# A scan with a feed-forward block behind it: matmuls dealt singly, a shorter start, and GpSimd in the preparation

## The chip, the cores and the metric

One NeuronCore of a Trainium2 chip. The metric is the device time of one execution in microseconds (us), the median over the runs shown.

## The reference

The input x has 16 sequences of 128 steps and 256 features. It drives a recurrence whose state q, p starts at cond. Each of the 128 steps is a Runge-Kutta step of fourth order, so each asks four times, one after the other, for the derivative:

```
def _derivative(q, p, drive, coupling, bias):
    i_couple = jnp.tanh(q) @ coupling.T
    dq = q - q ** 3 / 3.0 - p + drive + i_couple + bias
    dp = EPSILON * (q + ALPHA - BETA * p)
...
logits = x @ W_router.T                       # x is here the trace of q, 2048 tokens of 256
sh = _silu_and_mul(x @ Ws_gate_up, I_SH) @ Ws_down
gu = jnp.einsum('th,ehi->eti', x, We_gate_up)
h = _silu_and_mul(gu, I_MOE)
eo = jnp.einsum('eti,eih->eth', h, We_down)   # 8 experts, the two best weighted by softmax
```

The clipped q after every step is the token that goes through the feed-forward network (FFN): a shared part of 704 hidden columns and eight experts of 176. All are computed and weighted, and the sum is added to x.

## The kernel before

**Scan.** The 512 evaluations are called stages. 32 stages (8 steps) are a block; there are 16 blocks of 128 tokens. n counts stages over all blocks, st within one. In stage n TensorE (PE) runs `couple`: three small matmuls with a scaled identity add the three bf16 parts of x (line 554), eight multiply the high half of the coupling matrix and its rest by `th_hi` (565), and four use `th_lo` (571). ScalarE (ACT) makes `th_hi` and the float32 tanh (439, 440) from the new q; VectorE (DVE) subtracts them to `th_lo` (820), forms the cubic terms and `force`, and at line 848 adds PE's sum into the next q. That is a closed loop through the engines, 512 times.

**FFN.** The FFN of block f runs behind the scan of blocks f+1 and f+2. Tables name the stage at which each engine issues each piece. There are 17 tiles of 128 hidden columns. `UP_AT` gives two stages per tile: 6 matmuls for gate and 6 for up (629). ACT applies silu (`SILU_AT`, 480), DVE multiplies (`HIDE_AT`, 895), GpSimd (POOL) weights by the router's factor (`WEIGH_AT`, 963), PE multiplies with `w_down` (`DOWN_AT`, 646, two float32 matmuls per tile, four records in the trace). On PE this work stands between line 571 of one stage and line 554 of the next. A unit below is the time of one float16 matmul with 128 columns.

**Fillers.** `WARM` puts up to 6 matmuls whose result is not used (558) into a stage of the steady blocks that has fewer than 11 units. They stand between the x parts and the high half. In block 0, stages 16 to 18 have 8 fillers each (664), behind their coupling.

**Start.** SyncE (SP) issues all loads; DVE waits for `cf` and the identity, takes the largest coupling entry (690), PE turns it to one row (507), DVE reduces (692), PE widens it (511), five small DVE operations make a power of two `scale` and its inverse, two larger ones (713, 714) make the two float16 halves `c16`, and ACT and DVE prepare x of block 0 (394, 730, 734).

**Preparation of w_up.** During blocks 0 and 1 w_up is split into two float16 halves. `HI_AT` (ACT, line 417) makes the high half of a tile. The low half is either formed by DVE (`LO_AT`, 772) in rows of 128 columns (four rows a tile), or by PE and ACT: two matmuls per row give the rest in PSUM (`REST_AT`, 539 and 540) and ACT rounds it (`ROUND_AT`, 422). DVE does 9 tiles and PE with ACT 8.

**End.** After the last stage the FFN of block 15, and what is left of block 14, run in the same order without the scan between them. Then two additions and a store end the kernel.

Of the kernel before, what the change touches and what calls it, by code (L numbers as in the profile page):

```python
# [23 lines left out]
U32 = mybir.dt.uint32  # L24
ALU = mybir.AluOpType
# [47 lines left out]
def err(z):  # L73
# [13 lines left out]
UP_AT = [(2, 2), (3, 3), (4, 4), (6, 6), (8, 8), (9, 10), (11, 11), (12, 12), (13, 13), (15, 15), (16, 16), (17, 18),  # L87
         (20, 20), (22, 22), (23, 24), (26, 26), (27, 28)]
SILU_AT = [u[1] + 1 for u in UP_AT]
# [4 lines left out]
WEIGH_AT = [17, 18, 19, 21, 22, 23, 25, 26, 27, 29, 30, 31, 32, 37, 38, 39, 42]  # L94
# [3 lines left out]
assert len(UP_AT) == len(HIDE_AT) == len(DOWN_AT) == len(WEIGH_AT) == TILES and len(SPREAD_AT) == GROUPS  # L98
assert all(h > s for h, s in zip(HIDE_AT, SILU_AT))
assert all(w > max(s, c) and d > w for w, s, c, d in zip(WEIGH_AT, HIDE_AT, COPY_AT, DOWN_AT))  # L100
assert DOWN_AT[-1] < FINISH_AT[0] and FINISH_AT[-1] <= STAGES + DOWN_AT[0]


def units(st):

    halves = sum(u.count(st) for u in UP_AT)
    downs = DOWN_AT.count(st) + DOWN_AT.count(st + STAGES) + (st == 0)
    return 6 * halves + 8 * downs + 4 * SPREAD_AT.count(st)


WARM = [min(6, max(0, 11 - units(st))) for st in range(STAGES)]
# [5 lines left out]
HI_AT = {17: (0, 0, 4), 18: (1, 0, 4), 19: (2, 0, 4), 20: (3, 0, 4), 21: (4, 0, 4), 24: (5, 0, 4), 25: (6, 0, 4),  # L117
         28: (7, 0, 4), 29: (8, 0, 4), 30: (9, 0, 4), 33: (10, 0, 2), 37: (10, 2, 4), 38: (11, 0, 4), 41: (12, 0, 2),
         42: (13, 0, 4), 45: (12, 2, 4), 49: (14, 0, 2), 50: (14, 2, 4), 52: (15, 0, 4), 53: (16, 0, 4)}
REST_AT = {19: ((1, 0), (1, 1)), 20: ((1, 2), (1, 3)), 21: ((2, 0), (2, 1)), 22: ((2, 2), (2, 3)),  # L120
# [3 lines left out]
ROUND_AT = {22: 1, 23: 2, 26: 3, 27: 5, 31: 7, 34: 9, 40: 10, 47: 11}  # L124
REST_TILES = list(ROUND_AT.values())
LO_AT = {18: ((0, 0, 1),), 19: ((0, 1, 2),), 20: ((0, 2, 3),), 21: ((0, 3, 4),),
# [18 lines left out]
LO_DONE = {tile: so_far(LO_AT, n, i) for n, parts in sorted(LO_AT.items()) for i, (tile, _, _) in enumerate(parts)}
assert sorted([*LO_DONE, *REST_TILES]) == list(range(TILES))
assert sum(len(x) for x in REST_AT.values()) == ROWS * len(REST_TILES)
W_STEPS = 7
HALF = STEPS // 2
X_FIRST = [14, 15]  # L150
X_AT = [1, 3]
SPLIT_FIRST = [2, 5]
SPLIT_NEXT = [17, 19, 20]
SPLIT_AT = [20, 24, 28]
# [5 lines left out]
def program(nc, x, cond, coupling, bias, w_up, w_down, w_route, identity, spread, iota, e_base, out):  # L160
    ctx = ExitStack()
    with ctx:
# [33 lines left out]
        w_sum = sb("w_sum", [P, W_PARTS])  # L196
        most1 = sb("most1", [1, 2])
# [8 lines left out]
        p_first = sb("p_first", [P, KC, B])  # L206
# [46 lines left out]
        in_cf = sem("in_cf")  # L253
        in_core = sem("in_core")
        in_const = sem("in_const")
        in_x = sem("in_x")
# [4 lines left out]
        setup_a = sem("setup_a")  # L261
        zeroed = sem("zeroed")
        x_biased = sem("x_biased")
        x_split = sem("x_split")
# [8 lines left out]
        w_rounded = sem("w_rounded")  # L273

# [30 lines left out]
        SETUP_V = 12  # L305
# [23 lines left out]
        def _(sync):  # L329
            sync.dma_start(cf[:], coupling).then_inc(in_cf, 16)  # L330
            sync.dma_start(ident[:], identity).then_inc(in_cf, 16)
            sync.dma_start(bias_s[:], bias).then_inc(in_core, 16)
            sync.dma_start(xs[:, 0:STEPS], x[:, 0:STEPS]).then_inc(in_x, 16)
            sync.dma_start(q_raw[:], cond).then_inc(in_core, 16)
            sync.dma_start(q_trace[:, :, STEPS - 1, :], cond).then_inc(in_core, 16)
            sync.dma_start(p_first[:], cond).then_inc(in_core, 16)
            for i in range(ROWS):
                sync.dma_start(wf[:, i // 2, i % 2], w_up[:, i // 2, i % 2]).then_inc(in_w[i], 16)
            sync.dma_start(xs[:, STEPS:T], x[:, STEPS:T]).then_inc(in_x, 16)
# [684 lines left out]
```

## Time and profile before

| | |
|---|---|
| median of 3 runs | 655.67 us (655.66, 655.67 and 658.51) |
| the profiled execution, its own time | 658.68 us |
| its span, first to last instruction | 656.9 us |
| busy: PE, DVE, ACT, POOL | 97%, 93%, 56%, 30% of the span |
| mean granted TensorE clock | 0.992 |

Device time and span of the profiled execution differ by 1.8 us, which lie around the span. Busy time of PE counts overlapped matmuls whole, so 97% does not mean that PE could do no more: what a stage waits for is to be read from the order of starts.

### The profile page before, as it was taken

The numbers are of one execution on the slowest core, as the hardware profiler recorded it, in microseconds if no ns is written. First come the engines' busy times: TensorE is split into PE (matmuls) and PEld (weight loads), VectorE is DVE, ScalarE is ACT, GpSimd is POOL, SyncE is SP. The second block draws the span as 40 slices with busy tenths as digits, with TensorE's granted clock in tenths as the row PEclk, the third lists the DMA queues.
The fourth block names the chain that finished last, engine by engine and source line by source line (L and its number), as shares of the span: only waits on it lengthen the run. The fifth ranks groups of instructions, "written<-read, shape, count | busy, mean of one in ns | idle before, by whom it ended". The sixth has DMA issues, their size and how long they took to land.

```text
span 656.9 us, 33948 instructions
## 1 busy us (share of the span) xinstructions
PE 637.9 (97%) x12839; PEld 610.6 (93%) x12839; DVE 614.0 (93%) x4540; ACT 365.4 (56%) x1880; POOL 194.0 (30%) x436
## 2 busy tenths in 40 slices
PE   3899999999999999999999999999999999999998
PEld 2689899999999999999999999999999999999997
DVE  6998999999999999999999999999999999999951
ACT  4776655555555555556555555555556555554643
POOL 0002133242323334232333423233342323323244
PEclk9997999999999999999999999999999999999999
DMA  7800000000000000000000000000000000000000
GB/s 297 279 2 2 4 2 4 11 3 11 4 11 3 3 12 2 12 2 12 3 4 10 4 12 3 11 4 2 12 4 11 3 12 2 4 12 3 11 3 17
DMA packets 9059, 13.65 MB, mean 21 GB/s; under 512 B 1568, under 2 KB 8032, under 8 KB 8256
## 3 DMA queue, kind: packets, MB, share of 16 engines
q1 hardware_dynamic: 8896, 11.50, 5.2%
q8 instruction: 100, 1.64, 1.0%
q14 instruction: 63, 0.52, 0.3%
HBM read 9.40 MB, written 2.10 MB: 17 GB/s over the span
## 4 chain that ended last, share of the span: by engine, by line
PE 90%; DVE 8%; DMA 0%; issue 0%; ACT 0%; POOL 0%; DVEq 0%; SPq 0%
PE up_ps L629 28%; PE down_ps L646 21%; PE coup_ps L565 15%; PE coup_ps L571 13%; PE coup_ps L554 5%; PE coup_ps L558 3%; PE route_ps L603 2%; DVE q L848 1%; PE route_ps L584 1%; DVE w L772 1%; DVE force L831 1%; DVE th_lo L820 1%; DVE square_ps L817 1%; DVE square_ps L813 1%; DVE p_sum L784 1%; DVE y L784 0%
## 5 line engine op out<-in xcount | busy, mean ns | idle before, releaser
L629 PE MATMUL up_ps<-q_hi,w 128*128 128x128 f16 x2176 | 236.4, 219 | 0.2 <-POOL q_lo L926 0.2
L963 POOL TENSOR_TENSOR hidden<-hidden,comb_s 128x128 f32<-128x128 f32 x272 | 123.3, 456 | 297.7 <-ACT th_hi L439 290.2
L439 ACT ACTIVATE th_hi<-q 128x32 f16<-128x32 f32 x384 | 88.1, 229 | 213.6 <-DVE q L848 211.9
L629 PE MATMUL up_ps<-q_lo,w 128*128 128x128 f16 x1088 | 199.7, 220 | 0.0
L565 PE MATMUL coup_ps<-th_hi,c 128*128 128x16 f16 x4096 | 180.7, 171 | 0.2
L646 PE MATMUL down_ps<-hidden,wd 128*128 128x128 f32 x1088 | 180.8, 290 | 0.0
L629 PEld LDWEIGHTS up_ps<-q_hi,w 128*128 128x128 f16 x2176 | 176.2, 98 | 0.7 <-POOL q_lo L926 0.4
L565 PEld LDWEIGHTS coup_ps<-th_hi,c 128*128 128x128 f16 x4096 | 138.8, 96 | 4.6
L646 PEld LDWEIGHTS down_ps<-hidden,wd 128*128 128x128 f32 x1088 | 141.9, 191 | 0.0
L571 PE MATMUL coup_ps<-th_lo,c 128*128 128x16 f16 x2048 | 131.4, 173 | 0.4 <-DVE th_lo L820 0.3
L480 ACT ACTIVATE act_s<-up_ps,unscale 128x128 f32<-128x128 f32 x272 | 98.9, 364 | 13.8 <-PE up_ps L629 10.1
L629 PEld LDWEIGHTS up_ps<-q_lo,w 128*128 128x128 f16 x1088 | 105.9, 97 | 0.1
L554 PE MATMUL coup_ps<-xb,ident_u 128*128 128x32 bf16 x512 | 92.9, 181 | 10.1 <-DVE q L848 4.4
L571 PEld LDWEIGHTS coup_ps<-th_lo,c 128*128 128x128 f16 x2048 | 85.7, 97 | 16.2 <-DVE th_lo L820 0.7
L848 DVE SCALAR_TENSOR_TENSOR q<-coup_ps,c_un,force 128x32 f32<-128x32 f32 x384 | 96.3, 251 | 4.6 <-PE coup_ps L571 2.5
L820 DVE TENSOR_TENSOR th_lo<-th_ps,th_hi 128x32 f16<-128x32 f32 x512 | 97.8, 191 | 1.0 <-ACT th_ps L440 1.0
L554 PE MATMUL coup_ps<-x_rest,ident_u 128*128 128x32 bf16 x512 | 90.9, 178 | 0.0
L554 PE MATMUL coup_ps<-x_low,ident_u 128*128 128x32 bf16 x512 | 90.6, 177 | 0.0
L895 DVE TENSOR_TENSOR hidden<-act_s,up_ps 128x128 f32<-128x128 f32 x272 | 76.3, 281 | 13.2 <-ACT act_s L480 13.2
L813 DVE SCALAR_TENSOR_TENSOR square_ps<-q 128x32 f32<-128x32 f32 x384 | 76.6, 199 | 0.0
L817 DVE SCALAR_TENSOR_TENSOR square_ps<-square_ps,q 128x32 f32<-128x32 f32 x384 | 76.5, 199 | 0.0
L784 DVE SCALAR_TENSOR_TENSOR p_sum<-q,p_sum 128x32 f32<-128x32 f32 x384 | 71.0, 185 | 0.0
(107 smaller groups left out, 1098.8 us busy)
## 6 DMA issues: line engine op xcount, KB each, us to landing
wf<-in_w_up SPq DMA_DIRECT2D x4, 1056.0 KB, 8.3
wd<-in_w_down SPq DMA_DIRECT2D x1, 2048.0 KB, 21.0
out<-out_s SPq DMA_DIRECT2D x16, 128.0 KB, 2.2
xs<-in_x SPq DMA_DIRECT2D x1, 1920.0 KB, 17.3
sel<-in_spread SPq DMA_DIRECT2D x1, 408.0 KB, 17.1
cf<-in_coupling SPq DMA_DIRECT2D x1, 256.0 KB, 2.6
xs<-in_x SPq DMA_DIRECT2D x1, 128.0 KB, 2.4
ident<-in_identity SPq DMA_DIRECT2D x1, 64.0 KB, 2.5
```

Source lines behind the costliest of these rows:

```text
L439: nc.scalar.activation(th_hi[:], q[:], ACT.Tanh).then_inc(hi_ready, 1)
L480: nc.scalar.activation(act_s[:, j % 4, :], up_ps[(f * TILES + j) % UPS][:, 0:TOK], ACT.Silu, scale=unscale[:, 1:2]).then_inc(silu_ready, 1)
L554: nc.tensor.matmul(coup_ps[:, 0:CB], ident_u[:], piece, start=x == 0, stop=False, skip_group_check=True)
L565: nc.tensor.matmul(coup_ps[:, m * B:(m + 1) * B], c16[:, part, k, m * P:(m + 1) * P], th_hi[:, k, :], start=False, stop=False, skip_group_ ...
L571: last = nc.tensor.matmul(coup_ps[:, m * B:(m + 1) * B], c16[:, 0, k, m * P:(m + 1) * P], th_lo[:, k, :], start=False, stop=True, skip_gro ...
L629: last = nc.tensor.matmul(up_ps[(f * TILES + j) % UPS][:, h * TOK:(h + 1) * TOK], w16[:, part, k, h, j * P:(j + 1) * P], q[:, k, :], start ...
L646: last = nc.tensor.matmul(down_ps[:, m * TOK:(m + 1) * TOK], wd[:, j, m * P:(m + 1) * P], hidden[:, j, :], start=j == m == 0, stop=j == TI ...
L813: nc.vector.scalar_tensor_tensor(square, q, THIRD[k], q, ALU.mult, ALU.mult).then_inc(squared, 1)
L817: nc.vector.scalar_tensor_tensor(cubic, square, LINEAR[k], q, ALU.subtract, ALU.mult).then_inc(cubed, 1)
L820: nc.vector.tensor_tensor(th_lo[:], th, th_hi[:], ALU.subtract).then_inc(lo_ready, 1)
L848: nc.vector.scalar_tensor_tensor(q_raw[:] if k == 3 else q_in[k + 1][:], coup_ps[:, 0:CB].rearrange("p (m b) -> p m b", m=KC), c_un[:, (0, ...
L963: nc.gpsimd.tensor_tensor(hidden[:, j, :], hidden[:, j, :], comb_s[:, j, :], ALU.mult).then_inc(weighed, 1)
```

## The change

It has these parts.

1. `UP_AT` goes; `UPS_IN` says how many of the 204 up matmuls each stage issues, so a tile may begin or end within a stage. `DOWN_AT` gets a stage for each of the two down matmuls of a tile. Hide, spread and weigh stages move by a few places.
2. The fillers of the steady blocks and those of line 664 go. New ones stand at line 558 in stages 17 to 34 only: 10 minus 5 for each rest row of the stage before (and minus 8 for the router's stage), which is 10 at n = 17, 18, 21 and 22, 2 at n = 33, and none else.
3. The start: no turn and widen; one matmul of a matrix of ones with the row maxima gives a bound on them all. Three small operations for `scale` and its inverse. ACT loads cond and bias through its own queue, makes one half of the first `c16` part and the scaled identity; stage 0's tanh comes first. cond is loaded once instead of three times, and the identity is not waited for by the first reduction.
4. POOL splits x of blocks 0 and 1 into its three parts and adds the bias for blocks 1 and 2 (stages 1 to 13), which ACT and DVE did.
5. Low half of w_up: of 68 rows 36 come from PE and ACT (9 tiles), 23 from DVE, and 9 from POOL, which first makes the scaled row (`POOL_SCALE_AT`) and then subtracts (`POOL_LO_AT`). The rest rows of PE also use the bank `route_ps`.

```diff
-UP_AT = [(2, 2), (3, 3), (4, 4), (6, 6), (8, 8), (9, 10), (11, 11), (12, 12), (13, 13), (15, 15), (16, 16), (17, 18),
-         (20, 20), (22, 22), (23, 24), (26, 26), (27, 28)]
-HIDE_AT = [4, 7, 8, 10, 11, 12, 13, 14, 15, 18, 19, 21, 22, 25, 26, 29, 30]
+UPS_IN = [0, 0, 12, 8, 4, 8, 8, 8, 8, 8, 8, 8, 8, 10, 0, 11, 12, 8, 3, 8, 4, 8, 8, 8, 4, 8, 8, 8, 8, 0, 0, 0]
+HIDE_AT = [4, 7, 8, 10, 11, 12, 14, 15, 18, 19, 21, 22, 25, 26, 27, 29, 30]
-SPREAD_AT = [14, 17, 21, 25, 30]
+SPREAD_AT = [14, 17, 20, 24, 29]
-DOWN_AT = [18, 19, 21, 23, 24, 25, 27, 28, 29, 30, 31, 33, 37, 39, 41, 42, 46]
+DOWN_AT = [(18, 18), (19, 20), (21, 22), (23, 24), (25, 26), (27, 28), (29, 29), (30, 30), (31, 31), (31, 33),
+           (33, 35), (36, 36), (37, 38), (39, 40), (41, 42), (43, 44), (46, 46)]
...
-WARM = [min(6, max(0, 11 - units(st))) for st in range(STAGES)]
+WARM_FROM, WARM_TO = 17, STAGES + 3
+WARM = [max(0, 10 - 5 * len(REST_AT.get(n, ())) - 8 * (n == STAGES)) for n in range(WARM_TO)]
...
+REST_AT = {18: ((14, 0), (14, 1)), 19: ((14, 2), (14, 3)), 22: ((1, 0), (1, 1)), 23: ((1, 2), (1, 3)),
...
+           33: ((7, 0), (7, 1)), 35: ((7, 2),), 36: ((7, 3),), 38: ((10, 0),), 39: ((10, 1),), 40: ((10, 2),),
+           41: ((10, 3),), 42: ((13, 0),), 43: ((13, 1),), 44: ((13, 2),), 46: ((13, 3),)}
...
-         43: ((12, 0, 1),), 44: ((12, 1, 2),), 45: ((13, 0, 1),), 46: ((12, 2, 3),), 47: ((12, 3, 4),),
-         48: ((13, 1, 3),), 49: ((13, 3, 4),), 50: ((14, 0, 1),), 51: ((14, 1, 2),), 53: ((14, 2, 4), (15, 0, 1)),
-         54: ((15, 1, 2), (16, 0, 2)), 55: ((15, 2, 4), (16, 2, 4))}
+LO_AT = {17: (5, 0), 18: (5, 2), 19: (5, 3), 20: (8, 1), 21: (8, 2), 22: (8, 3), 23: (2, 1), 24: (2, 2), 25: (2, 3),
+         26: (0, 1), 27: (0, 2), 28: (0, 3), 29: (12, 0), 30: (12, 2), 31: (12, 3), 32: (11, 0), 41: (11, 2),
+         45: (11, 3), 48: (15, 0), 49: (15, 3), 52: (16, 1), 55: (16, 2), 56: (16, 3)}
+POOL_SCALE_AT = {17: (5, 1), 19: (8, 0), 22: (2, 0), 25: (0, 0), 27: (12, 1), 30: (11, 1), 37: (15, 2), 39: (15, 1),
+                 45: (16, 0)}
+POOL_LO_AT = {18: (5, 1), 21: (8, 0), 23: (2, 0), 26: (0, 0), 29: (12, 1), 31: (11, 1), 38: (15, 2), 42: (15, 1),
+              46: (16, 0)}
...
+X_AHEAD = {1: (0, 2), 2: (0, 3), 3: (1, "m0"), 5: (1, "m1"), 6: (1, 0), 7: (1, 1), 9: (1, 2), 10: (1, 3),
+           11: (2, "m0"), 13: (2, "m1")}
...
+            act.dma_start(q_raw[:], cond).then_inc(in_core, 16)
+            act.dma_start(bias_s[:], bias).then_inc(in_core, 16)
...
+                    act.wait_ge(setup_v, 4)
+                    nc.scalar.mul(c16[:, 0, 1], cf[:, 1], scale[:, 0:1]).then_inc(c_cast, 1)
+                    act.wait_ge(in_ident, 16)
+                    nc.scalar.mul(ident_u[:], ident[:], scale[:, 0:1]).then_inc(unit_cast, 1)
...
-            pe.wait_ge(in_cf, 2 * 16)
             pe.wait_ge(setup_v, 1)
-            turn(0).then_inc(setup_t, 1)
-            pe.wait_ge(setup_v, 2)
-            widen(0).then_inc(setup_t, 1)
+            nc.tensor.matmul(route_ps[:, 0:1], ones[:], most[:, 0:1], start=True, stop=True).then_inc(setup_t, 1)
...
-                if n > STAGES:
-                    for _ in range(WARM[st - 1]):
+                if WARM_FROM <= n < WARM_TO:
+                    for _ in range(WARM[n - 1]):
...
+                for i in range(UP_FROM[st], UP_FROM[st] + UPS_IN[st]) if st < STAGES else ():
+                    j, h, k, product = i // UP_MMS, i // (3 * KC) % 2, i // 3 % KC, i % 3
...
-                    if b == 0 and STAGES // 2 <= st < min(REST_AT):
-
-                        for _ in range(8):
-                            nc.tensor.matmul(up_ps[0][:, 0:P], c16[:, 0, 0, 0:P], c16[:, 0, 0, 0:P], start=True,
-                                             stop=True)
...
+            step(nc.vector.tensor_scalar(c16[:, 0, 0], cf[:, 0], scale[:, 0:1], None, ALU.mult))
+            step(rest_of_c(0))
+            dve.wait_ge(c_cast, 1)
+            step(rest_of_c(1))
...
+            split_x(0, 0)
+            split_x(0, 1)
+            pool.wait_ge(setup_v, 5)
...
+                    nc.gpsimd.tensor_scalar(w_scaled_row[:, 0:w.shape[-1]], w, scale[:, 1:2], None, ALU.mult
+                                            ).then_inc(w_pooled, 1)
...
+                    nc.gpsimd.tensor_tensor(w_lo, w_scaled_row[:, 0:w_lo.shape[-1]], w_hi, ALU.subtract
+                                            ).then_inc(w_pooled, 1)
...
+                    if n in X_AHEAD or n in POOL_SCALE_AT or n in POOL_LO_AT:
+
+                        pool.wait_ge(hi_ready, n + 1)
+                        prepare(n)
```

## Rows read from the trace of the kernel before

**Rows 1.** The page: the chain of work that ended last, by engine.

```profile
PE 90%; DVE 8%; DMA 0%; issue 0%; ACT 0%; POOL 0%; DVEq 0%; SPq 0%
```

**Rows 2.** The timeline (start us, duration us, engine, line, operation), two steady stages.

```profile
331.26 0.25 DVE L848 SCALAR_TENSOR_TENSOR q<-coup_ps,c_un,force 128x32 f32<-128x32 f32 x1
...
332.14 0.26 PE L571 MATMUL coup_ps<-th_lo,c 128*128 128x16 f16 x4
...
332.44 0.25 DVE L848 SCALAR_TENSOR_TENSOR q_raw<-coup_ps,c_un,force 128x32 f32<-128x32 f32 x1
...
333.65 0.25 DVE L848 SCALAR_TENSOR_TENSOR q<-coup_ps,c_un,force 128x32 f32<-128x32 f32 x1
```

**Rows 3.** The chain in order of time: twelve up matmuls, twice.

```profile
54.38 1.29 PE up_ps L629 x12
...
87.17 0.69 PE up_ps L629 x12
```

**Rows 4.** The timeline of PE alone: a stage with six ups and one tile of down.

```profile
335.76 0.25 PE L571 MATMUL coup_ps<-th_lo,c 128*128 128x16 f16 x4
...
336.20 0.66 PE L646 MATMUL down_ps<-hidden,wd 128*128 128x128 f32 x4
336.70 0.18 PE L554 MATMUL coup_ps<-xb,ident_u 128*128 128x32 bf16 x1
...
336.97 0.24 PE L571 MATMUL coup_ps<-th_lo,c 128*128 128x16 f16 x4
```

**Rows 5.** The timeline of DVE: q of stages 0, 30, 36, 63 and 511.

```profile
10.67 0.25 DVE L848 SCALAR_TENSOR_TENSOR q<-coup_ps,c_un,force 128x32 f32<-128x32 f32 x1
...
47.54 0.24 DVE L848 SCALAR_TENSOR_TENSOR q<-coup_ps,c_un,force 128x32 f32<-128x32 f32 x1
...
57.77 0.25 DVE L848 SCALAR_TENSOR_TENSOR q<-coup_ps,c_un,force 128x32 f32<-128x32 f32 x1 [0.41 <-PE coup_ps L571]
...
93.17 0.25 DVE L848 SCALAR_TENSOR_TENSOR q_raw<-coup_ps,c_un,force 128x32 f32<-128x32 f32 x1
...
628.81 0.25 DVE L848 SCALAR_TENSOR_TENSOR q_raw<-coup_ps,c_un,force 128x32 f32<-128x32 f32 x1
```

**Rows 6.** Windows of 1 us: start:end, length, busy of the engines, PEclk, DMA.

```profile
47.00:48.00 1.00, 1.00 (x17) 0.94 (x15) 1.00 (x9) 0.74 (x3) 0.00 (x0) 0.81 0.00 0
57.00:58.00 1.00, 1.00 (x25) 1.00 (x23) 0.59 (x6) 0.37 (x1) 0.30 (x1) 0.57 0.00 0
```

**Rows 7.** The timeline of the start.

```profile
3.67 0.69 DVE L690 TENSOR_REDUCE most<-cf 128x1 f32<-128x512 f32 x1 [1.93 <-DMA ident<-in_identity]
...
5.20 0.28 DVE L692 TENSOR_REDUCE most<-route_ps 1x1 f32<-1x128 f32 x1 [0.84 <-PE route_ps L507]
...
6.22 0.16 DVE L698 COPY most<-route_ps 128x1 f32<-128x1 f32 x1 [0.74 <-PE route_ps L511]
...
6.83 0.69 ACT L394 ACTIVATE xb<-xs,bias_c 128x128 f32<-128x128 f32 x2
...
7.16 0.49 DVE L713 TENSOR_SCALAR c<-cf,scale 128x512 f16<-128x512 f32 x1
...
7.68 0.75 DVE L714 SCALAR_TENSOR_TENSOR c<-cf,scale,c 128x512 f16<-128x512 f32 x1
```

**Rows 8.** The timeline of PE: fillers of stage 16 and what follows.

```profile
29.79 1.01 PE L664 MATMUL up_ps<-c 128*128 128x128 f16 x8
30.60 0.23 PE L554 MATMUL coup_ps<-xb,ident_u 128*128 128x32 bf16 x1
```

**Rows 9.** The timeline of PE: the last down matmuls.

```profile
649.98 3.79 PE L646 MATMUL down_ps<-hidden,wd 128*128 128x128 f32 x32
```

**Rows 10.** The timeline, then one line's instructions (min/median/max ns): POOL beside DVE.

```profile
82.63 0.46 POOL L963 TENSOR_TENSOR hidden<-hidden,comb_s 128x128 f32<-128x128 f32 x1 [1.22 <-ACT th_hi L439]
...
82.89 0.74 DVE L772 SCALAR_TENSOR_TENSOR w<-wf,scale,w 128x256 f16<-128x256 f32 x2
...
L772 DVE SCALAR_TENSOR_TENSOR w<-wf,scale,w x31: 343/345/479, 32.3 to 83.3; 128x128 f16<-128x128 f32 x28, 128x256 f16<-128x256 f32 x3
```

More of the change, by code:

```diff
@@ new lines, with in_order @@
+POOL_LO_AT = {18: (5, 1), 21: (8, 0), 23: (2, 0), 26: (0, 0), 29: (12, 1), 31: (11, 1), 38: (15, 2), 42: (15, 1),
+              46: (16, 0)}
+def in_order(table):
+    return [part for _, parts in sorted(table.items()) for part in parts]
+HI_ORDER = in_order(HI_AT)
+REST_ORDER = in_order(REST_AT)
+ROUND_ORDER = in_order(ROUND_AT)
+REST_TILES = list(REST_BANK)
+LO_ORDER = [part for _, part in sorted(LO_AT.items())]
+POOL_ORDER = [part for _, part in sorted(POOL_LO_AT.items())]
+assert POOL_ORDER == [part for _, part in sorted(POOL_SCALE_AT.items())]
@@ new lines, with rounds_done, parts_done, bank_rounds @@
+assert sorted(REST_ORDER + LO_ORDER + POOL_ORDER) == [(j, r) for j in range(TILES) for r in range(ROWS)]
+def hi_done(tile, row):
+    return max(i for i, (j, r0, r1) in enumerate(HI_ORDER) if j == tile and r0 <= row < r1) + 1
+def rounds_done(tile):
+    return max(i for i, part in enumerate(ROUND_ORDER) if part[0] == tile) + 1
+def parts_done(order, tile):
+    return max([i + 1 for i, part in enumerate(order) if part[0] == tile], default=0)
+def bank_rounds(bank):
+    return max(rounds_done(tile) for tile in REST_TILES if REST_BANK[tile] == bank)
@@ L545, in couple @@
                 if n == 0:
-                    pe.wait_ge(setup_v, 10)
+                    pe.wait_ge(setup_v, 3)
+                    pe.wait_ge(unit_cast, 1)
                 else:
@@ L561, in couple @@
                 pe.wait_ge(hi_ready, n + 1)
+                if n == 0:
+                    pe.wait_ge(setup_v, 6)
+                    pe.wait_ge(c_cast, 1)
                 for part in range(2):
+                    if n == 0 and part:
+                        pe.wait_ge(setup_v, 8)
                     for m in range(KC):
@@ L579, in ffn @@
                     pe.wait_ge(q_clipped, (f + 1) * STEPS)
-                    if not first_block:
+                    if first_block:
+                        pe.wait_ge(w_rounded, max(rounds_done(j) for j in REST_TILES
+                                                  if REST_BANK[j] == "route" and (j, 0) in REST_ORDER[:24]))
+                    else:
                         pe.wait_ge(comb_copied, f * TILES)
@@ L646, in ffn @@
+                for j in range(TILES):
+                    for m in range(KC):
+                        if DOWN_AT[j][m] == st:
+                            pe.wait_ge(weighed, f * TILES + j + 1)
+                            if j == m == 0:
+                                if first_block:
+                                    pe.wait_ge(w_rounded, bank_rounds("down"))
+                                else:
+                                    pe.wait_ge(out_ready, KC * f)
                             last = nc.tensor.matmul(down_ps[:, m * TOK:(m + 1) * TOK],
@@ L710, in _ @@
-            dve.wait_ge(setup_t, 2)
-            for x in range(5):
-                step(power(x, 0))
-            step(nc.vector.tensor_scalar(c16[:, 0], cf[:], scale[:, 0:1], None, ALU.mult))
-            step(nc.vector.scalar_tensor_tensor(c16[:, 1], cf[:], scale[:, 0:1], c16[:, 0], ALU.mult,
-                                                ALU.subtract))
-            step(nc.vector.tensor_scalar(ident_u[:], ident[:], scale[:, 0:1], None, ALU.mult))
-            for k in (0, 2, 3):
-                last = nc.vector.tensor_scalar(c_un[:, k:k + 1], unscale[:, 0:1], C[k], None, ALU.mult)
@@ L719, in _ @@
-            step(last)
-            dve.wait_ge(in_core, 4 * 16)
-            step(nc.vector.tensor_scalar(p_now[:], p_first[:], SHIFT, C[0] / Q_NEXT[0], ALU.subtract, ALU.mult))
-            assert done[0] == SETUP_V
+            dve.wait_ge(in_core, 2 * 16)
+            step(nc.vector.tensor_scalar(p_now[:], q_raw[:], SHIFT, C[0] / Q_NEXT[0], ALU.subtract, ALU.mult))
+            dve.wait_ge(tanh_ready, 1)
+            nc.vector.tensor_tensor(th_lo[:], th, th_hi[:], ALU.subtract).then_inc(lo_ready, 1)
@@ L768, in prepare @@
                                             ).then_inc(idents_ready, 1)
-                for j, r0, r1 in LO_AT.get(n, ()):
-                    dve.wait_ge(w_hi_ready, hi_done(j, r1 - 1))
-                    w, w_hi, w_lo = [x[:, r0:r1] for x in w_tile(j)]
+                if n in LO_AT:
+                    j, row = LO_AT[n]
+                    dve.wait_ge(w_hi_ready, hi_done(j, row))
+                    w, w_hi, w_lo = [x[:, row] for x in w_tile(j)]
                     nc.vector.scalar_tensor_tensor(w_lo, w, scale[:, 1:2], w_hi, ALU.mult, ALU.subtract
@@ L818, in scan_stage @@
                                                    ).then_inc(cubed, 1)
-                dve.wait_ge(tanh_ready, n + 1)
-                nc.vector.tensor_tensor(th_lo[:], th, th_hi[:], ALU.subtract).then_inc(lo_ready, 1)
-                if k == 0:
+                if n:
+                    dve.wait_ge(tanh_ready, n + 1)
+                    nc.vector.tensor_tensor(th_lo[:], th, th_hi[:], ALU.subtract).then_inc(lo_ready, 1)
+                if k == 0 and n:
                     dve.wait_ge(squared, n + 1)
```

311 lines of the change are left out of this document (178 added, 133 removed), and 11 rows, old and new, of tables (HI_AT, LO_AT, REST_AT).

## The prediction

> **What bounds the kernel now.** I read the page's chain first. It gives PE 90% [rows 1], which suggests that fewer or better packed matmuls pay everywhere. The timeline says otherwise. In a steady stage q starts at 331.26 and the next at 332.44, 1.18 us later; the one behind it, the first stage of a step, takes 1.21 [rows 2]. Within it PE's last four matmuls start at 332.14 and q 0.30 later. They had waited for th_lo, which comes through ACT and DVE from the q before. So the loop through three engines takes 1.18 whatever PE does in the gap, as long as PE is back in time. A step is 3 x 1.18 + 1.21 = 4.75 us, a block 38.0.
>
> How much PE may do in the gap: with six ups and one tile of down the period from line 571 to line 571 is 336.97 - 335.76 = 1.21, and there PE is the one that is late, by 0.03 [rows 4]. The down block took 0.50 of it (336.20 to 336.70). Twelve ups take 0.69, of which 0.02 is beyond twelve starts [rows 3], and leave the loop at 1.18: the stage from 331.26 to 332.44 comes behind twelve [rows 2]. So the limit lies near 0.80 us of work, 14 units, and the kernel is at it in a few stages per block.
>
> Then the times of q by stretch [rows 5]. Stage 0: 10.67. Stages 1 to 30: 36.87. Stages 31 to 36: 10.23. Stages 37 to 63: 35.40. The last 448 stages, 14 blocks: 535.64, or 38.26 a block. After the last q: 656.9 - 628.81 = 28.1. The windows of 1 us show why the third stretch is long: the granted clock falls at 47.6 to 0.50 (1.2 GHz) and is back at 57.9 [rows 6]; before it, PE had two stages with nothing but the coupling. Twelve ups cost 1.29 there instead of 0.69 [rows 3].
>
> **The change part by part.**
>
> *Start.* Now: largest entry at 3.67 for 0.69, first PE answer at 5.20 (0.84 after), second at 6.22, five small operations until 7.16 (0.19 each), 0.49 and 0.75 for the two halves [rows 7]. After: the reduction starts when cf is there; it was issued ahead of the identity, so I take 3.3 (bounds 2.9 and 3.67). It ends at 4.0, one PE answer at 4.85, two small operations, scale at 5.2, the third at 5.4. DVE casts half of c (0.26) and takes two halves of the rest (0.38 each): 6.45. PE's part and q follow 0.55 later: 7.0. Beside it: ACT has x with its bias 0.69 after its tanh, about 4.6; POOL's two splits, not seen before, I price at its 128x128 operation of 0.46 [rows 10]: 5.6; ACT casts and the scaled identity until 5.9. That cover is 0.4 to 0.8 us deep. Gain 10.67 - 7.0 = 3.7 (bounds 3.0 and 4.0; if POOL needed twice as long it would be 3.2). DVE's two x splits of stages 2 and 5 are gone too, 0.1.
>
> *Block 0 fillers.* Eight fillers cost 29.79 to 30.60, 0.81 at 1.2 GHz [rows 8], 0.10 each; at 2.4 GHz 0.057 [rows 3]. They used to stand behind the coupling, in the gap. The new ones stand between the x parts and the high half, that is on the loop. Ten cold ones end about 1.5 us after q where th_lo's matmuls used to start 0.88 after it [rows 2] and eight high-half matmuls (0.2) still have to come: +0.85 in stages 17 and 18 each, 1.7. The first rest rows at stage 18 are still partly cold: +0.4. At 21 and 22 the clock is up: ten take 0.57, +0.3 each, 0.6. Together 2.7. Today's block 0 has 36.87 against 35.6 for 30 undisturbed stages; some 0.6 of this are its 24 fillers. Net loss 2.1 (bounds 0.8, if the clock rises during stage 17, and 3.5, if it takes until 20).
>
> *The cold spell.* The new tables have rest rows or fillers in all but one stage from 17 to 33, so PE has no two empty stages; then come twelve ups. Stages 31 to 36 now cost 10.23; undisturbed 4 x 1.18 + 2 x 1.21 = 7.14. Gain 3.1, of which I leave 0.15 for ACT, which now rounds two halves at n = 33. So -2.95 against the profile (bounds 0 and 3.1).
>
> *Rest of block 1.* 35.40 for 27 stages against 32.0: 3.4 us are lost, because DVE's low rows (0.345 each [rows 10]) share stages with its hide operations and pile up at 53 to 55. After: eight DVE rows in block 1, none in a hide stage; single rest rows for PE beside 8 ups, 0.69/2 + 0.45 = 0.79, just at the limit; ACT at about 1.0 to 1.2 per stage. I leave 0.6 lost. Gain 2.75 (bounds 1.5 and 3.3). POOL's rows stand in stages where it had nothing.
>
> *Steady blocks.* The old fillers cost nothing: they stood in stages in which th_hi was not there yet. Their removal alone gives nothing. The even deal does: a stage now holds at most 12 ups or 8 ups and one down, 0.45 + 0.28 = 0.73 (half of 0.50, and 0.03 for changing over), under 0.80. 38.26 - 38.0 over 14 blocks is 3.3 us; I count five stages a block that are late by 0.03 as the one in rows 4, behind six ups and a tile of down, which is 2.1 of it, the rest are single late stages of another kind. Gain 2.2 (bounds 0.8 and 3.3). More is not to be had here, since the loop stays.
>
> *Tail.* No loop there; PE works without a gap until the last 32 records, which take 3.79 [rows 9], 0.114 each, 0.23 a down matmul. A block of 4 takes 0.50 [rows 4], so 0.05 is paid per change between ups and downs. After stage 511 block 14 has 15 down matmuls left instead of 12: +0.7. Single downs make 22 changes before the last up instead of 13: +0.4. Loss 1.1 (bounds 0.3 and 2.2).
>
> Sum: -3.7 - 0.1 + 2.1 - 2.95 - 2.75 - 2.2 + 1.1 = -8.5. Against the profiled execution: span 656.9 to 648.4, time 658.68 to 650.2.
>
> **The profile and the median.** The profiled execution is 3.0 us above the median, and one of the three runs (658.51) is at its height while two agree to 0.01. The only thing in the trace that costs 3 us at once is the cold spell, 3.1. I take it that the median run had none. Then the gain against the median lacks that term: 655.67 - (8.5 - 2.95) = 650.1. Both ways give the same time.
>
> **The rivals.** 0.5% of the time, about 3.3 us, is what a measurement can tell from no change.
>
> (a) The 3 us are the cost of being profiled, and the cold spell is in every run. Then 655.67 - 8.5 = 647.2. For it: profiled times stand above medians here. Against: 658.51 without a profile. Chance 0.13.
>
> (b) POOL and DVE get in each other's way. In 13 stages of blocks 0 and 1 both work on w_up; POOL starts when th_hi is ready and runs 0.46, DVE's low row starts 0.26 later [rows 10]; held up to POOL's end, q is 0.2 late in each: 2.6 us, 652.7. In the rows DVE's low rows started 0.26 into a POOL operation and took 0.74 for two; all 31 lie at 343 to 345 ns (479 for the double width), so nothing was held up. The Trainium skill, page "SBUF — State Buffer", section "Who interferes with whom", says that a DVE instruction with two SBUF inputs contends with a GpSimd instruction that reads SBUF, and that the loser waits for the whole instruction. By that rule the time would be this rival's; the trace does not agree. Chance 0.10.
>
> (c) The fillers come too late or too thin, and the clock stays at 1.2 GHz through block 0. Then ten stages with two rest rows each (0.69 warm, about 1.3 cold by the ratio of rows 3) cost 0.5 more each, and the first ups 3 more: 650.1 + 8 = 658, slower. Chance 0.05.
>
> (d) The clock falls in the steady blocks, where nothing fills a light stage any more. One fall costs 3.1. One is borne, two cancel the gain, from three on the kernel is slower; one per block would give 650 + 43 = 693. For it: stage 0 has only the router. Against: stages 29 to 1 hold about 12, 8, 12, 0 and 8 units beside the router where they now hold 8, 15, 8, 3 and 11, nearly as much, and it took two stages with the coupling alone to make it fall. Chance 0.07.
>
> **How the numbers follow.** The forecast, all terms as above, has 0.65; its own range, from the bounds of its terms taken one or two at a time, is 648 to 652.4, with 0.1 of it above 652.4. Faster by over 0.5% (under 652.4): 0.58 + 0.13 + 0.04 of (b) = 0.75. Slower by over 0.5% (over 658.9): most of (d) and half of (c), 0.09. Same: 0.16. The range that leaves no more than 2 in 10 out is 646.5 to 654.5: it takes in (a) and (b).
>
> **What would show it.** Start of q of stage 0 near 7.0. Stages 17 and 18 near 2.0 us, 21 and 22 near 1.5. PE clock 1.00 from stage 19 on, no fall near the turn of block 0. Stages 32 to 63 near 38.8 in all. Blocks 2 to 15 at 38.1. From the last q to the end 29.2. The sum is wrong if the steady blocks move by more than their 0.26, or if a 0.50 clock shows after stage 20.

## The result, and the profile after

The changed kernel takes 653.98 us, the median of 20 runs (650.95 to 661.84). The kernel before, run 20 times beside it, takes 658.5 (655.66 to 659.57). The ratio is 0.9937, 95% interval 0.9921 to 0.9952: faster by 0.6%. One run of the twenty, 661.84, counts as slow and is left out of the ratio. I had forecast 650.1, from 655.67 as the time before. The profiled execution took 656.32, with a span of 654.5; before it was 656.9. It lies 2.3 us above its own median.

The times of q in the changed kernel, stages 0, 30, 36, 63 and 511, from DVE's timeline, against [rows 5]:

```profile
7.36 0.25 DVE L907 SCALAR_TENSOR_TENSOR q<-coup_ps,c_un,force 128x32 f32<-128x32 f32 x1
...
50.96 0.24 DVE L907 SCALAR_TENSOR_TENSOR q<-coup_ps,c_un,force 128x32 f32<-128x32 f32 x1
...
58.32 0.25 DVE L907 SCALAR_TENSOR_TENSOR q<-coup_ps,c_un,force 128x32 f32<-128x32 f32 x1
...
90.80 0.24 DVE L907 SCALAR_TENSOR_TENSOR q_raw<-coup_ps,c_un,force 128x32 f32<-128x32 f32 x1
...
625.19 0.25 DVE L907 SCALAR_TENSOR_TENSOR q_raw<-coup_ps,c_un,force 128x32 f32<-128x32 f32 x1
```

| stretch | before | after | difference | forecast |
|---|---|---|---|---|
| until q of stage 0 | 10.67 | 7.36 | -3.31 | -3.7 |
| stages 1 to 16 | 19.32 | 20.26 | +0.94 | -0.1 |
| stages 17 to 30 | 17.55 | 23.34 | +5.79 | +2.1 |
| stages 31 to 36 | 10.23 | 7.36 | -2.87 | -2.95 |
| stages 37 to 63 | 35.40 | 32.48 | -2.92 | -2.75 |
| the last 448 stages | 535.64 | 534.39 | -1.25 | -2.2 |
| after the last q | 28.09 | 29.31 | +1.22 | +1.1 |
| span | 656.9 | 654.5 | -2.4 | -8.5 |

Four terms came out, the steady blocks gave half, and block 0 took back more than the start had given. Stages 17, 18, 21 and 22 take 1.98 to 1.99 us each and every stage from 19 to 26 that follows rest rows 1.76. PE's timeline shows why, first at stage 17, then at stages 25 and 26:

```profile
28.03 1.23 PE L601 MATMUL coup_ps<-c 128*128 128x128 f16 x10
29.05 0.41 PE L613 MATMUL coup_ps<-th_hi,c 128*128 128x16 f16 x8
29.31 0.25 PE L619 MATMUL coup_ps<-th_lo,c 128*128 128x16 f16 x4
29.91 0.21 PE L597 MATMUL coup_ps<-xb,ident_u 128*128 128x32 bf16 x1 [0.35 <-DVE q L907]
...
44.83 0.74 PE L577 MATMUL down_ps<-wf,ident_w 128*128 128x128 f32 x2
...
46.34 0.44 PE L577 MATMUL up_ps<-wf,ident_w 128*128 128x128 f32 x2
```

Ten fillers take 1.02 from start to start (28.03 to 29.05), and only then can the high half begin. The same float32 pair of a rest row takes 0.74 at 44.8 and 0.44 at 46.3: the clock was at 1.2 GHz until about 45.9. The windows don't show it:

```profile
30.00:31.00 1.00, 1.00 (x13) 1.00 (x14) 0.91 (x7) 0.85 (x3) 0.43 (x1) 1.00 0.11 34
45.00:46.00 1.00, 1.00 (x20) 0.94 (x19) 0.65 (x5) 0.59 (x1) 0.37 (x1) 1.00 0.00 0
```

PEclk reads 1.00 in both, though the matmuls of the first window have the durations of 1.2 GHz. In this trace the column says nothing until the first recorded change; the durations do. The trace of the kernel before is alike: PEclk is 1.00 from 30 to 31 us, while its fillers run at 0.10 each [rows 8]. So the mean clock of a run tells of later falls, not of how late the first rise came.

The other new loss stands at the start. DVE's first reduction begins at 3.46, ACT's sum over w_up waits at stage 1:

```profile
3.46 0.69 DVE L742 TENSOR_REDUCE most<-cf 128x1 f32<-128x512 f32 x1 [1.72 <-DMA cf<-in_coupling]
...
4.82 0.16 DVE L775 TENSOR_SCALAR ebits<-route_ps 128x1 uint32<-128x1 uint32 x1
...
5.78 1.02 DVE L788 SCALAR_TENSOR_TENSOR c<-cf,scale,c 128x256 f16<-128x256 f32 x2
...
8.95 0.79 ACT L445 ACTIVATE hidden<-wf 128x704 f32<-128x704 f32 x1 [0.99 <-DMA wf<-in_w_up]
```

The sum stands ahead of the next tanh in ACT's order. The scan starts 3.3 us sooner, the load of the first 1 MB of w_up is issued only 2.3 us sooner (2.13 against 4.41), and stage 2 takes 2.16 instead of 1.30.

### The profile page after: what moved, and what is told of

It is laid out like the page before. It is cut to its first block, busy times and chain, and to the rows that moved or that the text cites. A ratio compares the mean times of both kernels' runs of the same rounds, so it can differ in the third digit from the quotient of the medians.

```text
span 654.5 us, 33404 instructions
## 1 busy us (share of the span) xinstructions
PE 637.2 (97%) x12540; PEld 605.6 (93%) x12540; DVE 607.9 (93%) x4517; ACT 359.1 (55%) x1883; POOL 210.3 (32%) x468
## 4 chain that ended last, share of the span: by engine, by line
PE 95%; DVE 3%; DMA 1%; ACT 0%; issue 0%; SPq 0%; POOL 0%; DVEq 0%
PE up_ps L682 29%; PE down_ps L698 22%; PE coup_ps L613 17%; PE coup_ps L619 15%; PE coup_ps L597 6%; PE route_ps L657 3%; PE route_ps L636 1%; DMA wf<-in_w_up 1%; PE down_ps L577 1%; PE coup_ps L601 1%; DVE q L907 1%; PE route_ps L577 1%; PE up_ps L577 0%; DVE th_lo L875 0%; DVE w L830 0%
## 5 line engine op out<-in xcount | busy, mean ns | idle before, releaser
L698 PE MATMUL down_ps<-hidden,wd 128*128 128x128 f32 x1088 | 209.7, 296 | 0.0
L682 PE MATMUL up_ps<-q_lo,w 128*128 128x128 f16 x1088 | 202.8, 218 | 0.0
L682 PEld LDWEIGHTS up_ps<-q_hi,w 128*128 128x128 f16 x2176 | 167.6, 97 | 1.0 <-POOL q_lo L1040 0.4
L698 PEld LDWEIGHTS down_ps<-hidden,wd 128*128 128x128 f32 x1088 | 152.9, 191 | 0.0
L516 ACT ACTIVATE act_s<-up_ps,unscale 128x128 f32<-128x128 f32 x272 | 97.1, 357 | 8.8 <-PE up_ps L682 8.8
```

What stands on the lines that cost most here:

```text
L516: nc.scalar.activation(act_s[:, j % 4, :], up_ps[(f * TILES + j) % UPS][:, 0:TOK], ACT.Silu, scale=unscale[:, 1:2]).then_inc(silu_ready, 1)
L682: last = nc.tensor.matmul(up_ps[(f * TILES + j) % UPS][:, h * TOK:(h + 1) * TOK], w16[:, part, k, h, j * P:(j + 1) * P], q[:, k, :], start ...
L698: last = nc.tensor.matmul(down_ps[:, m * TOK:(m + 1) * TOK], wd[:, j, m * P:(m + 1) * P], hidden[:, j, :], start=j == m == 0, stop=j == TI ...
```

## The experiments

### Fillers out of the loop

```diff
-                if WARM_FROM <= n < WARM_TO:
-                    for _ in range(WARM[n - 1]):
-                        nc.tensor.matmul(coup_ps[:, 2 * P:3 * P], ...
...
+                    if n in (16, 17, 20, 21):
+                        for _ in range(WARM[n]):
+                            nc.tensor.matmul(up_ps[0][:, 0:P], c16[:, 0, 0, 0:P], c16[:, 0, 0, 0:P], ...
```

The new lines stand at the end of a stage on PE, behind its coupling.

> The changed kernel with its fillers (ten each, two of stage 32 left out) moved out of the loop, to the end of stages 16, 17, 20 and 21, behind the coupling. In the profile of the changed kernel stages 17, 18, 21 and 22 take 1.98 us each and all rest stages up to 26 take 1.76, because the clock comes up only at 45.9. Theory A (place): a cold filler block in the gap costs 0.25 and not 0.8 per stage, so stages 17, 18, 21 and 22 fall to about 1.45 (21 and 22 maybe 1.2), 2.0 us gained; the clock still comes late, about 652. Theory B (timing): what decides is when the clock comes up; if the place brings it up by stage 20, another 3 us go, about 649. Rival: without the fillers in the loop nothing changes, 654.

Measured: 651.23 (649.57 to 652.49, 6 runs), ratio to the kernel before 0.9906 (0.9885 to 0.9928). The profiled execution took 649.57 with a span of 647.8. Stages 17 to 30 take 17.58, against 23.34 in the changed kernel and 17.55 in the one before. PE's timeline:

```profile
26.86 1.23 PE L713 MATMUL up_ps<-c 128*128 128x128 f16 x10
28.33 1.23 PE L713 MATMUL up_ps<-c 128*128 128x128 f16 x10
29.79 0.72 PE L577 MATMUL up_ps<-wf,ident_w 128*128 128x128 f32 x2
30.41 0.44 PE L577 MATMUL up_ps<-wf,ident_w 128*128 128x128 f32 x2
```

The filler blocks now start 1.47 apart, not 1.98, and the clock is up at the second rest row, 3.5 us after the first filler. The profile bears theory B out: with the place the moment of the rise has changed too. A filler in the loop delays th_lo's matmuls and leaves PE idle while q, tanh and th_lo go round (from 29.56 to 29.91 in the first rows above); in the gap it fills that idle time. The two profiles exaggerate: by medians the place is worth 2.75 us, by the profiles 6.7. Two things vary between runs. Here the two runs with a mean granted clock of 1.000 took 649.57 and 649.89, the four with 0.997 took 651.20 to 652.49, so those four have a stretch at 1.2 GHz that this profile has not. In the changed kernel 15 of the 20 runs have 0.999 or 1.000 and still take 650.95 to 658.62. I take that to be the moment of the first rise; there is only one profile, so it is not shown.

### No fillers, a run of fillers, fewer fillers

```diff
-                    if n in (16, 17, 20, 21):
-                        for _ in range(WARM[n]):
+                    if 14 <= n <= 17:            # a_run_fill
+                        for _ in range(10):
...
+                        for _ in range(6):       # g_six, stages 16, 17, 20, 21
```

> The changed kernel with no fillers at all. Theory A (the fillers do not bring the clock up, the rest rows do): stages 17, 21 at 1.20, rest stages cold at 1.76 until about the same time, so some 3 us less than the changed kernel, 651. Theory B (the fillers are needed): the clock stays at 1.2 GHz through the rest rows into the first ups of block 1, ten rest stages and six up stages cold, 3 us of fillers saved and 3 or more lost, 654 to 658.

Measured: 656.61 (652.56 to 658.25, 12 runs), ratio 0.9972 (0.9950 to 0.9994). In the profile all stages from 23 to 30 take 1.73 to 1.76. With rest rows alone the clock does come up, but at stage 30:

```profile
49.96 0.78 PE L577 MATMUL up_ps<-wf,ident_w 128*128 128x128 f32 x2
50.63 0.49 PE L577 MATMUL up_ps<-wf,ident_w 128*128 128x128 f32 x2
```

And it is down again for stages 34 and 35, the first ups (1.65 and 1.67). So it comes up before the first ups and not behind them, as theory B had it, but by medians the kernel is 2.6 us slower than with fillers on the loop and 5.4 slower than with them in the gap: they are needed.

> The changed kernel with ten fillers behind the coupling in each of stages 14 to 17, one run of float16 matmuls right ahead of the first rest rows, as the kernel before had it with three times eight. Theory B (an unbroken run of float16 work brings the clock up, broken fillers and float32 rest rows do not): clock up by stage 18 or 19, four stages at about 1.45 and all rest stages at 1.2; span near 649, time near 650.5, and little spread between runs. Theory A (the moment is chance): stages 18 to 25 still cold in the profile, 653.

Measured: 655.78 (651.02 to 658.99, 12 runs), ratio 0.9962 (0.9939 to 0.9985). My expectation missed. The run did bring the clock up: stages 19 and 20, behind rest rows, take 1.20. But stages 20 and 21 have neither rest rows nor fillers now, and from stage 23 to 28 it is 1.53 to 1.76 again, down as in a_no_fill. A run ahead of the work does not last over two empty stages. The twelve runs agree: the one with a mean clock of 1.000 took 651.02, the two with 0.979 took 658.44 and 658.99. Stage 15 also takes 2.17, since the fillers behind stage 14 start late, at 25.20, after a small matmul of the preparation that stands there, and push the next coupling back to 26.24.

> The changed kernel with six fillers instead of ten behind the coupling of stages 16, 17, 20 and 21. If the fillers' amount decides, the clock comes up late again (rest stages at 1.76) and the time is 653 to 656 with a wide spread. If the unbroken order of work decides and not the amount, stages 17 and 18 take 1.2 to 1.25 instead of 1.45 and the time is 0.5 less than with ten, 650.7.

Measured: 651.08 (650.03 to 656.47, 6 runs), ratio 0.9918 (0.9886 to 0.9949). In the profile stages 17 and 18 take 1.42 and 1.22, but 19 and 20 are cold (1.74, 1.76); behind the rest rows of stage 22 it is 1.20. The median is that of ten fillers, the upper end is 4 us higher. It looks as if fewer fillers cost less and leave more to chance, but six runs each do not show it.

This profile has one more thing that no other profile of the changed kernel or its variants has: the clock falls in the steady blocks, at stage 163, and two stages take 1.77 and 1.45.

```profile
203.32 0.25 DVE L908 SCALAR_TENSOR_TENSOR q<-coup_ps,c_un,force 128x32 f32<-128x32 f32 x1
205.09 0.25 DVE L908 SCALAR_TENSOR_TENSOR q_raw<-coup_ps,c_un,force 128x32 f32<-128x32 f32 x1 [0.60 <-PE coup_ps L615]
206.54 0.25 DVE L908 SCALAR_TENSOR_TENSOR q<-coup_ps,c_un,force 128x32 f32<-128x32 f32 x1 [0.18 <-PE coup_ps L615]
```

Its steady tables are those of the changed kernel, and stage 163 is the fourth stage of block 5. So a fall near the turn of a block can happen there too; it cost 0.8 us.

### The deal and the steady fillers, each alone

Three kernels built on the kernel before: the new deal of FFN work with the old fillers kept, the old deal without the fillers of line 558, and the new deal without them.

```diff
-                if n > STAGES:                   # b_no_warm, b_deal_no_warm
+                if False:
                     for _ in range(WARM[st - 1]):
...
-UP_AT = [(2, 2), (3, 3), ...                     # b_deal, b_deal_no_warm
+UPS_IN = [0, 0, 12, 8, 4, ...
-DOWN_AT = [18, 19, 21, ...
+DOWN_AT = [(18, 18), (19, 20), ...
+WARM = [3, 3, 0, 0, 0, 3, 0, 3, 0, 0, 0, 0, 0, 0, 0, 0, 0, 1, 0, 3, 0, 0, 0, 0, 0, 0, 0, 0, 0, 3, 0, 3]
```

> The kernel before with only the new deal of FFN work (ups singly, a stage for each down matmul, new hide, spread and weigh places); its start, its preparation of w_up and all its fillers stay. My terms: steady blocks -2.2 (the two profiles together say -1.3), tail +1.1 (they say +1.2), so -1.1 to +0.2 against the kernel before. Rival: the deal is worth more and the steady gain is hidden in the changed kernel by something else, -3.

> The kernel before without its steady fillers (line 558), nothing else. My prediction says they cost nothing, since they stand where th_hi is not there yet: 0 +- 0.3 in the last 448 stages (535.6) and the clock stays up. Rival: they cost, as the new deal with the old fillers (536.96) against the new deal without them (534.0 to 534.4) suggests, up to 2.5 us, so 533; then half of the change's steady gain is the removal. Second rival: the clock falls now and then, +3 us or more per fall.

> The kernel before with the new deal and without its steady fillers: the fourth corner. Old deal with fillers took 535.6 us for the last 448 stages, old deal without 545.0, new deal with 537.0. Theory: with the even deal the clock holds by itself and the fillers only delay the high half, so 534.0 to 534.5 here as in the changed kernel, no window of 1.2 GHz after block 2; against b_deal 2.6 us less, about 659. Rival: the changed kernel's steady blocks hold the clock for another reason (its start or preparation), and this one falls at block turns as the old deal did, 540 or more.

| | the last 448 stages | after the last q | median | ratio to before |
|---|---|---|---|---|
| old deal, fillers (before) | 535.64 | 28.1 | 658.5 | 1 |
| old deal, no fillers | 544.96 | 28.1 | 667.04 (5 runs) | 1.0135 (1.0116 to 1.0155) |
| new deal, fillers | 536.96 | 29.3 | 661.67 (6 runs) | 1.0063 (1.0044 to 1.0083) |
| new deal, no fillers | 533.31 | 29.4 | 657.07 (12 runs) | 0.9977 (0.9964 to 0.9989) |

The first two expectations missed: the deal alone costs 3 us instead of gaining up to 1.1, and without its fillers the old deal is 9.3 us longer in these stages, the second rival. The third held, and gained 1 to 2 us more than expected. The stretch times are of one profile each, differences of rows like these, q of stages 63 and 511 with the new deal without fillers:

```profile
92.64 0.25 DVE L842 SCALAR_TENSOR_TENSOR q_raw<-coup_ps,c_un,force 128x32 f32<-128x32 f32 x1
...
625.95 0.25 DVE L842 SCALAR_TENSOR_TENSOR q_raw<-coup_ps,c_un,force 128x32 f32<-128x32 f32 x1
```

The four corners tell more than the change as a whole. Without its fillers the old deal loses the clock at the turn of most blocks; the page of that kernel, 40 slices of the span, and windows of 1 us at the turn to block 4:

```profile
PEclk9998999989798999989899898999989899998999
```

```profile
170.00:171.00 1.00, 1.00 (x17) 0.83 (x14) 0.97 (x9) 0.72 (x4) 0.25 (x2) 0.85 0.05 16
171.00:172.00 1.00, 1.00 (x15) 0.98 (x16) 0.92 (x9) 0.44 (x3) 0.42 (x1) 0.50 0.00 0
...
176.00:177.00 1.00, 1.00 (x22) 1.00 (x19) 0.60 (x5) 0.68 (x3) 0.01 (x1) 0.50 0.08 16
178.00:179.00 1.00, 1.00 (x18) 0.85 (x18) 0.94 (x9) 0.38 (x3) 0.35 (x1) 1.00 0.00 0
```

and q on DVE in that stretch, 1.68 us apart where 1.18 and 1.21 are usual:

```profile
173.04 0.25 DVE L848 SCALAR_TENSOR_TENSOR q<-coup_ps,c_un,force 128x32 f32<-128x32 f32 x1 [0.33 <-PE coup_ps L571]
174.72 0.25 DVE L848 SCALAR_TENSOR_TENSOR q_raw<-coup_ps,c_un,force 128x32 f32<-128x32 f32 x1 [0.52 <-PE coup_ps L571]
176.40 0.25 DVE L848 SCALAR_TENSOR_TENSOR q<-coup_ps,c_un,force 128x32 f32<-128x32 f32 x1 [0.40 <-PE coup_ps L571]
```

Ten of the fourteen blocks have a stage over 1.4 us among their stages 2 to 5; the fillers are worth 9.3 us there. With the even deal they are worth less than nothing: stages 0, 6, 8 and 20 take 1.297, 1.261, 1.269 and 1.265 on average where without them they take 1.212, 1.180, 1.211 and 1.209, 0.28 us a block, because three fillers now follow a stage with 12 units where the old table had 8, and hold back the high half. In the profile without fillers the clock stays up all the same from 57.0 us until the scan has ended. So the deal is what makes the removal possible, and the removal is what makes the deal pay. Neither is a gain alone: the deal by itself is slower by 0.6%, the removal by 1.35%.

### The wait at stage 2, and pairs in the tail

```diff
+                if i == 0:
+                    sync.dma_start(wf[:, 0, 0, 0:W_COLS], w_up[:, 0, 0, 0:W_COLS]).then_inc(in_w_first, 16)
+                cols = slice(0 if i else W_COLS, F)
...
-                    act.wait_ge(in_w[part // 3], 16)
+                    act.wait_ge(in_w[part // 3] if part else in_w_first, 16)
```

> The changed kernel with fillers in the gap, and the first third of w_up's first row loaded by a transfer of its own ahead of the rest. In the changed kernel ACT waits 0.99 us at stage 1 for that row (1 MB) and stage 2 takes 2.16. Theory: the third (352 KB) lands some 1.5 us sooner, stage 2 falls to 1.20 to 1.30, -0.9 us. Rival: the wait moves to the next third at stage 2 or to the next row, no gain.

Measured: 650.85 (649.04 to 651.79, 4 runs), ratio 0.9883 (0.9860 to 0.9906). Stage 2 takes 1.27; in six profiles without the split it took 1.38 to 2.16, so the transfer's own time varies from run to run. By stage 2 the expectation holds; a difference in the median of 0.4 is within its spread. Part of the rival holds too: at stage 10 ACT now waits 0.32 us for a later row of w_up, and stage 11 takes 1.41 instead of 1.20.

```diff
+                        pair = tail and (f == BLOCKS - 1 or DOWN_AT[j][0] >= STAGES)
-                        if DOWN_AT[j][m] == st:
+                        if DOWN_AT[j][1 if pair else m] == st:
```

> The changed kernel with fillers in the gap; after the last stage the two down matmuls of a tile are issued together again. My term says 0.05 us per change between float16 and float32 work, 9 changes fewer: 29.3 falls to 28.9 from the last q to the end; the other 0.7 (three down matmuls left over) stay. Rival: changes cost nothing, 29.3.

Measured: 650.28 (649.63 to 650.95, 4 runs), ratio 0.9880 (0.9859 to 0.9901). From the last q to the end 649.1 - 620.09 = 29.0, against 647.8 - 618.47 = 29.3: the changes between float16 and float32 cost 0.3, a little less than my 0.4. The two profiles below, which have the pairs too, give 29.1.

### Together

> The changed kernel with fillers in the gap (ten behind stages 16, 17, 20, 21), the first third of w_up loaded ahead, down matmuls in pairs after the last stage, and three fillers each in stages 32 to 34 ahead of the high half, against the cold spell at stages 34 and 35 that two of the last four profiles show (1.7 us each instead of 1.2). Expected: no such spell, 649.5; rival: the spell stays, 650.3 as before.

> As h_best with ten more fillers behind stage 15. They cost 0.25 us; if they bring the clock up before stage 18 in every run, up to 1.1 us of cold rest stages go (two profiles of four had them): 649.2 and a narrow spread. If the run before stage 18 was long enough already, 649.8.

Measured: 649.66 (649.27 to 651.83, 6 runs), ratio 0.9873 (0.9853 to 0.9893), and with stage 15 filled too 649.63 (649.39 to 649.74, 5 runs), ratio 0.9865 (0.9845 to 0.9885). The edits are those above, and

```diff
+                if STAGES <= n < STAGES + 3:
+                    for _ in range(3):
+                        nc.tensor.matmul(coup_ps[:, 2 * P:3 * P], ...
...
-                    if n in (16, 17, 20, 21):
+                    if n in (15, 16, 17, 20, 21):    # h_best15
```

No stage in either profile is cold at stages 34 and 35 (1.24 and 1.18). One run of h_best, 651.83, has a mean clock of 0.997 where the others have 1.000, so a stretch at 1.2 GHz still occurs; the five runs of h_best15 have 0.999 or 1.000. h_best15's profile has a wait for w_up at stage 10 as above, 0.54 us, and stage 11 takes 1.63. With five filler blocks stages 18 to 30 take 1.20 to 1.23 and five runs lie within 0.35 us, where the changed kernel's runs spread over more than 7. q of stages 0, 30 and 511:

```profile
7.43 0.25 DVE L918 SCALAR_TENSOR_TENSOR q<-coup_ps,c_un,force 128x32 f32<-128x32 f32 x1
...
44.76 0.24 DVE L918 SCALAR_TENSOR_TENSOR q<-coup_ps,c_un,force 128x32 f32<-128x32 f32 x1
...
618.73 0.25 DVE L918 SCALAR_TENSOR_TENSOR q_raw<-coup_ps,c_un,force 128x32 f32<-128x32 f32 x1
```

Stage 30 comes 6.2 us sooner than in the changed kernel's profile. This version beats both kernels: 1.35% under the one before, and by the medians 4.35 us under the changed one.

## Why the prediction was right or wrong

**The time before.** I took 655.67 for a run without the cold spell, and that reading is borne out: in 23 further runs of the kernel before, the three with a mean granted clock of 1.000 took 655.70 to 655.76, and the ten with 0.992, the clock of the profile, 658.57 to 660.12. What failed is the step from three runs to the median: most runs have the spell, and the median is 658.5. Of rival (a), the spell was in most runs and not in every one; the 3 us as a cost of being profiled was wrong. The forecast of 650.1 came out the same by both ways, so this error made the forecast gain too small and did not move the forecast time.

**Block 0 fillers.** "Net loss 2.1 (bounds 0.8 ... and 3.5, if it takes until 20)". This is the step that failed, and the main one. The size per stage was right: 1.98 for stages 17, 18 against "near 2.0". The moment at which the clock rises was wrong: about 45.9, stage 26, not by stage 19. Every rest stage until then cost 0.56 more, and stages 21 and 22 cost 0.8 instead of 0.3. The net is +5.8 in the profile, past my bound. I had rival (c) for it and gave it 0.05, with the clock down into block 1 as well; half of it happened in the profile, and by their times less in most other runs. I had no row for the moment and took it for granted that fillers on the loop raise the clock as those in the gap had; a_gap_fill, with the same four blocks of ten in the gap, has the clock up 3.5 us after the first and behind twenty of them. My sign for this, a 0.50 clock after stage 20, does not show in the column, as said above; the durations show it.

**The cold spell.** Right in size, -2.87. But two of the four profiles with fillers in the gap and none at stages 32 to 34 have it, at stages 34 and 35, and a_no_fill has it too, so the changed tables do not rule it out; in those two it costs 1.0 us and is shorter than in the profile before.

**The rest of block 1.** -2.92 against -2.75. The stage times are 1.17 to 1.32, where stages 43 to 51 took up to 1.42 and stages 53 to 55 up to 1.81 before. That fits the low rows out of the hide stages; no run takes this part of the change by itself.

**The start.** -3.31 against -3.7. PE's answer came at 4.82 as worked out. The two rest halves of c took 0.49 each, not 0.38, and the cast of a half 0.35, not 0.26: I had halved 0.75 and 0.49, but half the width does not cost half (line 788 has 1.02 for the two). I had also priced at nothing what the earlier scan runs into, the load of w_up: 0.9 at stage 2 of the profile. That a faster start makes the next load late is the plain omission.

**POOL.** Rival (b) is refuted. POOL works on w_up beside DVE and nothing is held up; in stage 26:

```profile
44.94 0.43 POOL L1032 TENSOR_TENSOR w<-w_scaled_row,w 128x128 f16<-128x128 f32 x1 [1.14 <-ACT th_hi L475]
...
45.20 0.34 DVE L830 SCALAR_TENSOR_TENSOR w<-wf,scale,w 128x128 f16<-128x128 f32 x1
```

All 20 rows of full width have at most 347 ns, as before [rows 10]. The rule of the Trainium skill's page "SBUF — State Buffer", section "Who interferes with whom", would have held DVE's row until 45.37; the trace does not agree.

**Steady blocks.** Forecast -2.2, profile -1.25; b_deal_no_warm gives -2.33. The gain that I had counted is there: stages 11, 19, 25 and 29 of a block average 1.210, 1.209, 1.212 and 1.211 before and 1.181, 1.181, 1.182 and 1.181 in the changed kernel. What is missing lies in single late stages: the changed kernel's profile has 11 stages more than 0.06 above 1.18 (1.21 for the first stage of a step), 1.7 us together, the one before 6, 1.0 us. They are not chance. The same eleven, stages 90, 104, 117, 132, 158, 172, 199, 335, 362, 485 and 498, are late in all nine profiles that have the new start and preparation. In nine of these stages of the changed kernel q follows the start of th_lo's matmuls by 0.35 to 0.59 instead of 0.30, so it is DVE that is late. At stage 335 of the changed kernel DVE idles before its hide operation with nothing in the profile that it waits for:

```profile
415.26 0.29 DVE L954 TENSOR_TENSOR hidden<-act_s,up_ps 128x128 f32<-128x128 f32 x1 [0.24 <-issue]
```

Why it does so is open. "The old fillers cost nothing ... Their removal alone gives nothing" was half wrong: it gives nothing and costs 9.3 us. I had set rival (d), the clock falling in the steady blocks, at 0.07, from a comparison of units at the block's turn. The comparison was of the right two kernels, and for the changed kernel's profile its answer was right; g_six shows that a fall is possible. Its price was not 3.1 but 0.8 there. That the old deal needs its fillers I had not seen, nor that the new deal could not bear them.

**The tail.** +1.22 against +1.1; the part for changes 0.2 to 0.3 against 0.4.

What stays open: what sets the moment at which the clock rises. Work without a break is not enough. In a_no_fill PE last idles before 35.17 us, then does rest rows and coupling with no idle time that the profile shows, and is at 1.2 GHz until about 50.7:

```profile
35.17 0.21 PE L597 MATMUL coup_ps<-xb,ident_u 128*128 128x32 bf16 x1 [0.36 <-DVE q L903]
```

From the last idle time to the rise it took 15.5 us there, 8.6 in the changed kernel (37.4 to 46.0), 8.9 in g_six, 4.9 in the kernel before and 4.2 in a_gap_fill. In that time a_no_fill has no filler, the changed kernel ten, and g_six two groups of twelve with the rest rows of two stages between them; the kernel before has 24 in one group and a_gap_fill twenty. No run changes the kind of work alone, and how far the moment varies from run to run is seen in the times only.

## What to carry to other kernels

Filler matmuls are work with a place: ten of them on the loop added 0.8 us to a stage, in the gap 0.25, and there the clock came up 16 us sooner. On the loop only as many are cheap as fit into a wait that is there anyway: three behind a stage with 8 units hold the clock of the old deal, three behind a stage with 12 only delay it. When a change has two halves that lean on each other, run all four combinations before either is judged; here each half alone is slower and both together are faster. When a start is made shorter, price the next thing that the earlier work will meet, and take more than three runs before reading a state of the kernel into their median.

## What the runs showed of the hardware

The same rest rows in float32, without fillers, needed from stage 18 to stage 30, some 20 us with two empty stages in between, until the clock rose, the last 15.5 us of them with no idle time of PE in the profile; twenty float16 fillers in the gap and one rest row needed 3.5. Two stages with nothing but the coupling, after a run of fillers, let it fall (a_run_fill: a float32 pair takes 0.44 at 32.3 and 0.74 at 36.1). So did the turn of a block, in ten of fourteen blocks, in the old deal without fillers, whose stages 29 to 1 hold 8, 12, 8, 8 and 8 units (the router as 8); with the new deal's 12, 8, 12, 8 and 8 it fell once in the ten profiles without steady fillers. A DVE operation of line 788's kind took 0.75 us at width 512 [rows 7], 0.49 at 256 and 0.34 at 128. On POOL a 128x128 multiplication by a per-partition scalar took 0.60 to 0.67 us and a subtraction 0.40 to 0.50.
